# Audio tower on one core: weight loads, products and rows moved in the order tables of a Mamba and MLP kernel

## The reference

```python
h = tok(x)                                   # patches @ W.T + b
h = h + attn(layernorm(h))
h = h + ffn(layernorm(h))

# attn: res = x; x = rmsnorm(x)
z, xv, B, C, dt_in = split(x @ in_proj_w.T)  # 1024, 256, 256, 1024, 128
dt = softplus(dt_in @ dt_proj_w.T + b)
hstate = exp(dt * A) * hstate + dt * x * B   # over the sequence, 16 states a channel
y = (C * hstate).sum(states) + D * x
h = res + (y * silu(z)) @ out_proj_w.T
h = h + (silu(hn @ gate.T) * (hn @ up.T)) @ down.T      # hn = rmsnorm(h)
# ffn: the same gated MLP, 512 -> 2048 -> 512, after a layernorm
```

## Time and profile before

| | |
|---|---|
| median of 3 runs | 665.3 us (664.75 to 665.99) |
| the profiled execution | 665.3 us, its span 663.5 us |
| PE busy | 627.1 us (95% of the span) |
| DVE, ACT, POOL busy | 416.9, 341.9, 429.0 us |
| DMA, mean rate | 246 GB/s |
| mean granted clock of PE | 0.985 |

### The profile page before, as it was taken

The page is one execution under the profiler, slowest core; times in us unless marked ns, Lnnn a source line. Parts: engine busy times, 40 slices in busy tenths (PEclk is TensorE's granted clock), DMA queues, the critical chain, the costliest instruction groups (busy, mean ns, idle before and its releaser), DMA issues.

```text
span 663.5 us, 8621 instructions
## 1 busy us (share of the span) xinstructions
PE 627.1 (95%) x2846; PEld 501.8 (76%) x2846; DVE 416.9 (63%) x531; ACT 341.9 (52%) x768; POOL 429.0 (65%) x244
## 2 busy tenths in 40 slices
PE   5779998999995999999998999999999999999998
PEld 4547665666663767777765777766999998999998
DVE  4097887998877899888898888842232222332232
ACT  4368987488985564333374433413543443643440
POOL 0376766476777999987789987544465563455461
PEclk9959999999998999999999999999999999999999
DMA  8899996599999779988969998544244344244421
GB/s 334 305 372 344 304 328 231 189 356 347 329 362 395 279 250 367 412 332 308 323 223 312 402 326 315 171 127 159 96 133 151 103 154 127 66 144 136 131 68 44
DMA packets 49164, 163.50 MB, mean 246 GB/s; under 512 B 4320, under 2 KB 18528, under 8 KB 48480
## 3 DMA queue, kind: packets, MB, share of 16 engines
q1 hardware_dynamic: 49120, 162.95, 70.5%
HBM read 145.24 MB, written 17.69 MB: 246 GB/s over the span
## 4 chain that ended last, share of the span: by engine, by line
PE 76%; DVE 13%; issue 4%; ACT 3%; DMA 2%; POOL 1%; DVEq 0%; SPq 0%; ACTq 0%; POOLq 0%
PE work L1013 54%; PE da L1013 16%; DVE da L799 7%; PE work L1023 6%; DVE hs L809 3%; ACT L535 1%; DMA b_rows<-sq 1%; ACT da L561 1%; DMA bb<-b_rows 1%; DVE sq L883 1%; DMA sm<-small 1%; POOL hs L460 0%; DVE work L824 0%; DVE sq L899 0%; DVE a L892 0%
## 5 line engine op out<-in xcount | busy, mean ns | idle before, releaser
L799 DVE TENSOR_TENSOR_SCAN da<-da,hs 128x580 f32<-128x580 f32 (+1 forms) x128 | 191.1, 1493 | 35.0 <-POOL hs L460 19.2
L460 POOL TENSOR_TENSOR hs<-dtx,bb 128x1160 f32<-128x1160 f32 (+1 forms) x64 | 171.3, 2677 | 58.1 <-PE work L1023 43.7
L439 POOL TENSOR_TENSOR ws<-wraw,ws 128x1024 fp32r<-128x1024 f32 x40 | 101.3, 2534 | 92.9 <-ACT ws L570 92.9
L1013 PE MATMUL work<-sq,wraw 128*128 128x290 f32 x512 | 127.0, 407 | 3.8 <-DVE gate L952 2.6
L1013 PEld LDWEIGHTS work<-sq,wraw 128*128 128x128 f32 x512 | 96.1, 189 | 34.4 <-issue 4.8
L561 ACT ACTIVATE da<-dt,a_neg 128x261 f32<-128x261 f32 (+1 forms) x256 | 118.3, 494 | 0.0
L809 DVE TENSOR_TENSOR hs<-da,cb 128x580 f32<-128x580 f32 (+1 forms) x128 | 105.3, 823 | 15.3 <-DMA cb<-c_rows 6.8
L1013 PE MATMUL work<-hn,win 128*128 128x290 f32 (+1 forms) x336 | 98.7, 442 | 12.3 <-ACT c_rows L644 6.9
L1013 PEld LDWEIGHTS work<-hn,win 128*128 128x128 f32 x336 | 63.7, 192 | 41.9 <-issue 16.3
L558 ACT COPY da<-zeros 128x58 f32<-128x58 f32 (+1 forms) x128 | 27.7, 217 | 128.8 <-DVE hs L809 128.6
L570 ACT CAST ws<-wraw 128x1024 fp32r<-128x1024 f32 x48 | 50.3, 1049 | 70.4 <-PE da L1013 34.4
(11 more groups left out here) (103 smaller groups left out, 645.5 us busy)
## 6 DMA issues: line engine op xcount, KB each, us to landing
wraw<-w_stream SPq DMA_DIRECT2D x104, 512.0 KB, 4.0
bb<-b_rows SPq DMA_DIRECT2D x32, 700.0 KB, 7.5
cb<-c_rows SPq DMA_DIRECT2D x32, 700.0 KB, 5.9
bb<-b_rows SPq DMA_DIRECT2D x32, 580.0 KB, 8.5
cb<-c_rows SPq DMA_DIRECT2D x32, 580.0 KB, 6.7
c_rows<-c_rows SPq DMA_DIRECT2D x8, 875.0 KB, 10.6
c_rows<-c_rows SPq DMA_DIRECT2D x8, 725.0 KB, 7.1
win<-w_in SPq DMA_DIRECT2D x4, 1024.0 KB, 13.8
```

The lines of the kernel that those rows point to most:

```text
L439: nc.gpsimd.tensor_tensor(ws[:, k % NW, 1, :], wraw[:, split_loads[k] % NRAW, :], ws[:, k % NW, 0, :].bitcast(F32), ALU.subtract).then_inc ...
L460: nc.gpsimd.tensor_tensor(hs[:, u % NH, 0:NQ * n].rearrange("p (n t) -> p n t", t=n), dtx[:, t % 2, 0:n].unsqueeze(1).to_broadcast([P, NQ, ...
L799: nc.vector.tensor_tensor_scan(da[:, j, 0:w], da[:, j, 0:w], hs[:, u % NH, j * w:(j + 1) * w], 0.0, ALU.mult, ALU.add).then_inc(scan_done, 1)
L1013: last = nc.tensor.matmul(dst, w, x, start=(k == 0), stop=(k == len(pairs) - 1))
```

## The change

Four things, all in the order tables:

- `FIRST_LOADS` gives each of the first six weight loads its own place in SP's list and its own product to wait for. They go out beside units 15, 17, 18, 19, 24 and 25.
- `in_c(1,5)` leaves unit 27. It and `in_c(1,6)` are the fillers before and after the mean of `rms2(0)`, each one after the other; `in_z(1,7)` goes to unit 33, behind `xs(1,7)` and ahead of the outputs.
- ACT loads the tanh table at the end of the slots of `rms2(0)` and of `ln2_var(0)`; before, it did so only for `rms2(0)` and otherwise at the first tanh.
- In the prologue `in_b(0,0)` and `in_b(0,1)` come ahead of `in_dt(0)`; the waits for the norm's parts go to the first of them.

```diff
+FIRST_LOADS = [(("dtp", 0, 7), ("mean", 1)), (("in_x", 1, 1), ("in_x", 1, 0)), (("in_b", 1, 0), ("in_x", 1, 1)),
+               (("in_b", 1, 1), ("in_c", 1, 0)), (("in_z", 1, 0), ("in_z", 1, 0)), (("in_c", 1, 2), ("in_c", 1, 2))]
...
-    in_c = [("in_c", c, k) for k in (m, m + 1) if (c, k) != (0, 1)]
+    in_c = [("in_c", c, k) for k in (m, m + 1) if (c, k) not in ((0, 1), (1, 5))]
...
-    slots = [(None, [("bmean", 0), *tokens(0), ("mean", 0), ("ln1", 0), ("rms1", 0), ("in_dt", 0), ("in_b", 0, 0), ("in_b", 0, 1),
+    slots = [(None, [("bmean", 0), *tokens(0), ("mean", 0), ("ln1", 0), ("rms1", 0), ("in_b", 0, 0), ("in_b", 0, 1), ("in_dt", 0),
...
-    first = [[], [("xs", 1, 7)], o[0:2], o[2:4]]
+    first = [[], [("xs", 1, 7), ("in_z", 1, 7)], o[0:2], o[2:4]]
...
-        rest += {"rms2": [("in_c", 1, 6), s, ("in_z", 1, 7)], "ln2_mean": [s, ("dtp", 1, 7)],
+        rest += {"rms2": [("in_c", 1, 5), s, ("in_c", 1, 6)], "ln2_mean": [s, ("dtp", 1, 7)],
...
-SEAM = (("in_c", 1, 6), ("in_z", 1, 7), ("dtp", 1, 7), ("in_c", 1, 7))
+SEAM = (("in_c", 1, 5), ("in_c", 1, 6), ("dtp", 1, 7), ("in_c", 1, 7))
...
-                if i == 0:
-                    full(sp, ("in_z", 1, 2))
+                if i < NRAW:
+                    full(sp, FIRST_LOADS[i][1])
...
-                    if s == ("in_z", 1, 2):
-                        for i in range(NRAW):
+                    for i, (at, _) in enumerate(FIRST_LOADS):
+                        if s == at:
                             load_w(i)
...
                 if tables[0] == "silu_and_others" and unit is not None:
-                    use_tables("exp_and_others" if ("rms2", 0) in steps else "natural_log_exp_and_others")
+                    log_tables()
+                if ("rms2", 0) in steps or ("ln2_var", 0) in steps:
+                    if unit is not None:
+                        use_tables("exp_and_others")
...
-                    ready = [(norm_done, KD * v + k + 1) if kind == "in_dt" else () for k in range(KD)]
+                    head = s in (("in_b", 0, 0), ("in_dt", 1))
+                    ready = [(norm_done, KD * v + k + 1) if head else () for k in range(KD)]
```

## The result

The changed kernel takes **662.25 us** (median of 6 runs, 661.64 to 663.24), the kernel before, timed beside it, 665.12 (664.75 to 666.17). The ratio is 0.9955, with an interval of 0.9942 to 0.9968: 2.9 us faster. The profiled execution took 661.94 us, its span is 660.0 (before 663.5). That is inside the range and faster, as forecast, but 1.75 us short of the 660.5. The gain came at the places that the forecast names, and nearly in its sizes; two terms put at 0 cost something.

What follows compares the result with a forecast made beforehand. It took PE to carry the end, its 7.09 us hole before chunk 0's output projection traced to C loads behind six weight loads; 3.85 + 1.0 + 0 + 0 = 4.85 us off 665.3 gave 660.5, range 657.8 to 663.8 us.

Steps and rivals of the forecast that it cites:

- The two stalls on rows of C, and the gate: DVE, units 31 and 32: 6.7 us of C waits go, ACT then binds, chunk 0's last gate ends 4.2 us earlier.
- seam: Units 31 to 37, from the end of chunk 0's recurrence into its outputs: forecast gain 3.85 us.
- Rival 1: ACT does not bind at 198 us, all 6.7 us return at the gate: 657.9 us; chance 0.15.
- The new bank wait: Before out(0,1): the turned bank is emptied late by ACT, so PE waits 2.5 us amid the outputs.
- rival 3: The hole only moves: longer bank wait or half clock at out(0,0), 1.4 us lost, 661.9 us; chance 0.12.
- The outputs: Chunk 0's output projection: ends at 227.45 us against 231.3, a gain of 3.85 us.
- `in_c(1,5)` gone from unit 27: Unit 27: without this product PE is 2.36 us earlier at the third silu's wait.
- The table: ACT after chunk 0's second norm: tanh table loaded ahead, 1.28 us a load, tanh, gate and PE 1.0 us earlier.
- The loads one by one: Six weight loads behind C loads of units 15 to 25: cost taken as 0, bounds 0 and 1.5 us lost.
- Rival 2: SP's queue, units 17 to 28: spread loads stall DVE up to 6 us, 666.5 us, chance 0.08; half, 0.1.
- The prologue: Kernel start: B 0.3 us earlier, C store 0.75 later, first product unchanged; taken as 0, bounds -0.9 and +0.75 us.

Runs made afterwards that it cites:

- loads_only: The kernel before with only the six weight loads at their new single places; 662.09 us, ratio 0.9956.
- moves_only: Kernel before with only in_c(1,5) out of unit 27 as a filler and in_z(1,7) ahead of the outputs, six loads in one block; 664.27 us, ratio 0.9984.
- after_again: The changed kernel itself, unedited, for a second profiled execution; 662.08 us, ratio 0.9949.
- prologue_only: The kernel before with only in_dt(0) put behind the two products for rows of B; 665.94 us, ratio 1.0005.

## Why the prediction was right, and where it was off

- **The two stalls on rows of C, and the gate** (forecast 4.2 us earlier): 4.34, the same within 0.01 in all nine profiles with loads and moves. The figure it is compared with is less firm: against the mean of three profiles of the old seam it is 4.2. That ACT's decays, not C, would then set unit 31's second scan was right (1.74 us). Rival 1 (all 6.7 us back) did not come.
- **The new bank wait** (2.5 us): 2.46 at full clock, 0.77 when the clock fell. It hid the slow first output, as rival 3 had it; but the 1.4 us that rival 3 feared on top did not come. It had counted 3.9 us more for an output at half clock throughout; the clock was back before the output's end, it took 1.7 us more (5.84 against 4.15), and 5.84 us still ended before the bank was free. That the kernel lost nothing by the fallen clock is the bank's doing, not the forecast's, which had the outputs at full clock.
- **The outputs** gave back 0.76 instead of 0.35 (4.2 less 3.85). The end came out late by 0.2 for the second output's start (6.6 us behind the first, not 6.4) and 0.2 for the three that follow (11.98 against 11.8). Seam: 3.58 us against 3.85.
- **The cause inside the seam was incomplete.** The step "`in_c(1,5)` gone from unit 27" counted PE's 2.36 us and not the 875 KB store that leaves SP's queue with it. It changed no sum, since in `loads_only`, which keeps the store and has no block, no issue from 182 to 196 us takes more than 0.56 us; it is why `moves_only` missed.
- **The table** (1.0 us): 1.02. The Trainium skill (ScalarE: Activation LUTs, What ACT_TABLE_LOAD costs) gives about 2.66 us a switch with a drain; the next operation here starts 0.02 us after the 1.28, and 1.02 us came back and not 2.3, so the measurement decides against the drain in this place.
- **The loads one by one** (0, with up to 1.5 lost): the first term that was mis-sized, 0.67 us in the mean of eight profiles, though -0.04 in the change's first. The step took one landing of 8.6 us as the slack of all; the profiles show that landings in this stretch scatter by more than the slack: the same kernel waited once for C in its first profile and at least four times in its second. Rival 2 was right as a mechanism, far below its price.
- **The prologue** (0, bounds -0.9 and +0.75): the step that failed. It dated the C store 0.75 us later and then looked only at unit 0's first product. Queued behind the first C load is the B load of unit 1; DVE's wait before unit 1's first scan went from 0.53 to 2.16 us and stayed in all of chunk 0: the shift at unit 20 is +1.19, 1.0 of it beyond the 0.2 us that PE's first product came later. The C store itself went out 1.27 us later (24.77 against 23.50), not 0.75. By the pairs of runs the cost is between 0 and 1.4; how much of the 1.0 is the order and how much the execution stays open.

Sum with the measured terms: 3.58 + 1.02 - 0.67 = 3.9 us (4.4 with the seam against the mean of three), less the prologue's; the timed gain is 2.9. That leaves 1.0 to 1.5 us for the prologue, at the upper end of what the pairs allow. This remainder takes up every other error and is no measurement of its own.

## What to carry to other kernels

A moved step must be followed through every queue in which it leaves something or out of which it takes something: here a store behind PE's product, and a B load behind a C load, decided more than the product itself. Try the parts alone, too: by the timed runs one of the four (the loads) made up the whole gain here, and the others cancelled within the noise. Where a queue carries bulk loads beside loads with a deadline, spread them, but ask for slack against the scatter of the landings and not against one of them. And when work is put into a hole ahead of a consumer, look at who empties the buffers that the new order hands to that consumer.

## What the runs showed that I had not expected

- The clock after a hole is not a property of the kernel. In two profiles of the same program the first output took 5.84 us behind 2.72 us of idle PE and 4.15 behind 2.92. PE in `after_again`:

```profile
210.84 4.15 PE L1020 MATMUL work<-yg,wraw 128*128 128x290 f32 x16 [2.92 <-issue]
217.45 11.98 PE L1020 MATMUL work<-yg,wraw 128*128 128x290 f32 x48 [2.46 <-ACT xf L664]
```

Of seven profiles with a hole of 2.7 to 2.9 us, four fell to half clock (first output 5.54 to 5.84 us) and three did not. The Trainium skill (TensorE: Matmul & The Clock Gate, Part 1: The HAM clock gate) says that the number of slow products at a kernel's start differs from run to run of one kernel; here the same is seen in mid-kernel.
- An issue on SP can be long, and all that stands behind it waits: that of one B load took 4.84 us at 188.06 before, behind six weight loads and a store of 875 KB, against 0.52 to 0.56 for those in `loads_only` from 182 to 196 us. That the full queue is the cause is argued, not shown.
- The landing of the first B load of unit 1, from issue, was 7.3 us in the change and about 4.8 in `prologue_only` (30.28 to 35.04), with the same transfers ahead of it. Why is open.
